# Routing of the first experts: row tables as single-row operations, work moved behind the ids, first hidden product moved ahead of the shares

## The reference

```
x = x + xattn(layernorm(x), ctx, mask)       # 16 heads, 77 context rows, 2048 tokens, width 256
h = layernorm(x)
scores = sigmoid(h @ gate.T + bias)           # 9 experts
top_scores, selected = top_k(scores, 2); top_scores /= sum(top_scores)
out = x + sum_e cw[:, e] * ((silu(h @ w1[e].T) * (h @ w3[e].T)) @ w2[e].T)   # hidden width 704
```

## Time and profile before

| what | value |
| --- | --- |
| median of 3 runs | 422.93 us (422.58 to 423.85) |
| profiled execution: own time | 422.82 us |
| its span (first to last instruction) | 421.0 us |
| mean granted PE clock | 0.989 |
| busy share of the span | PE 96%, DVE 65%, ACT 60%, POOL 59% |

### The profile page before, as it was taken

One profiled execution on the slowest core, in us unless ns is written; L12 is line 12 of the kernel. 1 busy time (PEld: TensorE's weight loads), 2 busy tenths in 40 slices (PEclk: granted clock), 3 DMA queues, 4 the chain that ended last, 5 costly groups with the idle time before them and its releaser, 6 DMA issues.

```text
span 421.0 us, 10140 instructions
## 1 busy us (share of the span) xinstructions
PE 403.9 (96%) x3176; PEld 307.2 (73%) x3176; DVE 275.2 (65%) x683; ACT 253.2 (60%) x444; POOL 246.9 (59%) x214
## 2 busy tenths in 40 slices
PE   8999999999999999789899999999999999999991
PEld 7777677778877877776677777777777777777781
DVE  1777989999899988987889854444444444444430
ACT  3759899999999986724655444444444444444430
POOL 6536789998999888253245534445444444444232
PEclk9999999999999999989999999999999999999997
DMA  7994456576575666256789978989889989989742
GB/s 228 342 321 132 132 160 201 161 189 201 155 235 166 177 187 190 74 151 120 154 138 139 146 131 133 141 139 129 150 141 142 141 139 140 143 134 153 119 68 36
DMA packets 106512, 66.03 MB, mean 157 GB/s; under 512 B 80992, under 2 KB 99808, under 8 KB 106464
## 3 DMA queue, kind: packets, MB, share of 16 engines
q1 hardware_dynamic: 98784, 54.90, 57.4%
q0 software_dynamic: 7680, 10.49, 16.5%
HBM read 36.23 MB, written 9.96 MB: 110 GB/s over the span
## 4 chain that ended last, share of the span: by engine, by line
PE 56%; issue 16%; DMA 14%; DVE 4%; POOLq 4%; POOL 3%; SPq 1%; ACT 0%; DVEq 0%
PE ps L824 12%; PE ps L621 12%; PE ps L651 11%; DMA out_rows<-work,idx_all 9%; PE ps L844 7%; PE ps L634 4%; POOLq L1709 3%; PE ps L558 3%; POOL work L1700 3%; PE ps L617 2%; DMA w_all<-in_wv 2%; PE ps L523 1%; DMA work<-work 1%; PE ps L667 1%; DMA work<-xn_rows,idx_all 1%
## 5 line engine op out<-in xcount | busy, mean ns | idle before, releaser
L824 PE MATMUL ps<-w_all,work 128*128 x960 | 150.1, 313 | 0.8 <-DVE work L1447 0.5
L824 PEld LDWEIGHTS ps<-w_all,work 128*128 128x128 f16 x960 | 93.6, 98 | 47.0 <-issue 1.2
L1721 POOL DMA_INDIRECT out_rows<-work,idx_all x40 | 64.2, 1606 | 102.5 <-ACT work L1076 101.1
L1516 DVE SCALAR_TENSOR_TENSOR work<-ps,work 128x352 f32<-128x352 f32 x80 | 41.2, 523 | 66.4 <-PE ps L824 66.3
L844 PE MATMUL ps<-w_all,work 128*128 x681 | 80.8, 273 | 1.1 <-DMA work<-work 1.1
L844 PEld LDWEIGHTS ps<-w_all,work 128*128 128x128 f16 x681 | 66.3, 98 | 12.0 <-issue 1.6
L1641 POOL TENSOR_TENSOR w_all<-stage,w_all 128x1088 f16<-128x1088 f32 x31 | 69.9, 2256 | 6.5 <-ACT w_all L916 6.2
L1055 ACT ACTIVATE work<-ps 128x352 f32<-128x352 f32 x80 | 36.8, 463 | 53.6 <-PE ps L824 53.6
L1061 ACT ACTIVATE work<-work 128x704 f16<-128x704 f32 x39 | 30.8, 790 | 62.2 <-DVE work L1516 62.2
L1700 POOL DMA_INDIRECT work<-xn_rows,idx_all x40 | 40.6, 1014 | 29.9 <-issue 10.3
L621 PE MATMUL ps<-w_all 128*128 128x462 f16 (+1 forms) x288 | 57.4, 336 | 0.0
(11 more groups left out here) (159 smaller groups left out, 537.2 us busy)
## 6 DMA issues: line engine op xcount, KB each, us to landing
stage<-in_wt SPq DMA_DIRECT2D x36, 544.0 KB, 4.4
work<-in_x SPq DMA_DIRECT2D x30, 128.0 KB, 3.7
out_rows<-work SPq DMA_DIRECT2D x18, 128.0 KB, 4.3
xn_rows<-work SPq DMA_DIRECT2D x18, 128.0 KB, 4.1
w_all<-in_x SPq DMA_DIRECT2D x1, 1536.0 KB, 14.6
work<-work SPq DMA_TRANSPOSE x78, 3.6
w_all<-in_wq SPq DMA_DIRECT2D x4, 256.0 KB, 6.8
w_all<-in_wv SPq DMA_DIRECT2D x2, 512.0 KB, 8.2
```

Source lines behind the costliest of these rows:

```text
L824: mm = pe.matmul(ps[:, c, 0:half], xt[:, t % 2, block, :], weights(wbase + off, half), start=(k == 0 and n == 0), stop=(k == KD - 1 and n ...
L1516: dve.scalar_tensor_tensor(out=sg[:, t % 2, cols], in0=ps[:, 2 + c, 0:HID // 2], scalar=1.0 / SP_W, in1=sg[:, t % 2, cols], op0=ALU.mult, ...
L1721: pool.indirect_dma_start(out=acc, out_offset=bass.IndirectOffsetOnAxis(ap=idx_all[:, t:t + 1], axis=0), in_=yb[:, t % 2], in_offset=None, ...
```

## The change

Five edits, all between the end of the attention loop and the third expert tile:

1. The 22 rows of `vhot1` are written by 22 `tensor_scalar` operations of 128 elements, each compared with a scalar per partition, in place of two `tensor_tensor` operations of 1408 elements. `pi` is first copied to a float table `pif`.
2. The two one-hot operations of `experts_of` become one of twice the width (both routings).
3. `stats` and `aggregate` of tile 13 go from ahead of `first_slots` to behind `ids_of(0)`; `normalise2(13)` goes behind `aggregate(14)` and the first `w_rest`, `rstd(13)` goes behind the gathers of tiles 0 and 1 in POOL's queue. `logits(11)` goes behind `residual(14)`.
4. On PE `gate_turn(12)` goes behind `first_ids`, `gate_logits(12)` into `project(15)`, `gate_turn(13)` behind `project(15)`, `gate_logits(13)` into up(0); ACT's `gate_copy(12)` goes behind the two table loads, `gate_copy(13)` behind `first_high`. The fillers become 8, 0 and 26 in place of 30, 16 and 10.
5. On DVE `normalise2(15)` and `shares(0)` go behind `hidden(0)`, and `logits(13)` ahead of step 0.

```diff
@@ PE
-        WARM, WARM_IDS, WARM_OUT, WARM_X0 = 30, 30, 16, 10
+        WARM, WARM_IDS, WARM_X0 = 30, 8, 26
...
                     if i == NT - 1 and c == G_AT:
-                        gate_turn(NT - 3)
+                        gate_logits(NT + 1 - LAG_G)
...
                 prob_turn(NT - 1)
-                gate_turn(NT + 1 - LAG_G)
                 pe.wait_ge(sub_ok, 3 * NT)
                 warm(WARM_IDS, WARM_LATE)
                 first_ids()
-                gate_logits(NT + 1 - LAG_G)
-                warm(WARM_OUT, WARM_LATE)
+                gate_turn(NT + 1 - LAG_G)
                 project(NT - 1)
-                gate_logits(NT - 3)
+                gate_turn(NT - 3)
...
-                if s in (1, 2):
+                if s in (0, 1, 2):
                     gate_logits(NT - 3 + s)
@@ ACT
-            gate_copy(NT + 1 - LAG_G)
             sigmoids(0, K1)
             act.activation(mx[:, 0, 0:1], eps[:], ACT.Silu)
+            gate_copy(NT + 1 - LAG_G)
+            first_high()
             gate_copy(NT - 3)
-            first_high()
@@ DVE, experts_of
-                for k in range(2):
-                    ins = dve.tensor_tensor(oh[:, k], by_expert(con[:, C_IOTA:C_IOTA + E9], n),
-                                            idx[:, k].unsqueeze(2).to_broadcast([P, n, E9]), ALU.is_equal)
-                link(ins)
+                link(dve.tensor_tensor(oh, by_expert(con[:, C_IOTA:C_IOTA + E9], n).unsqueeze(1).to_broadcast([P, 2, n, E9]),
+                                       idx.unsqueeze(3).to_broadcast([P, 2, n, E9]), ALU.is_equal))
@@ DVE, first_rows
+                dve.tensor_copy(r["pif"][:, :, 0:K1], r["pi"][:, :, 0:K1])
...
                 for k in range(2):
-                    row_hot(vhot1[:, k * K1:(k + 1) * K1, :], r["pi"][:, k, 0:K1], K1).then_inc(v1_ok, 1)
+                    for i in range(K1):
+                        ins = dve.tensor_scalar(vhot1[:, k * K1 + i, :], iota16[:], r["pif"][:, k, i:i + 1], None, ALU.is_equal)
+                    ins.then_inc(v1_ok, 1)
@@ DVE, drain
-                stats(NT - 3)
-                aggregate(NT - 3)
                 first_slots()
-                logits(NT - LAG_G)
                 first_rows()
                 residual(NT - 2)
+                logits(NT - LAG_G)
                 first_index()
                 p_low(NT - 1)
                 ids_of(0)
-                normalise2(NT - 3)
+                stats(NT - 3)
+                aggregate(NT - 3)
                 logits(NT + 1 - LAG_G)
                 stats(NT - 2)
                 aggregate(NT - 2)
                 w_rest(4 * EARLY + 3)
+                normalise2(NT - 3)
                 w_rest(4 * E9 - 4)
                 first_low()
-                logits(NT - 3)
@@ DVE, fstep
                     normalise2(NT - 2)
-                if n == 0:
-                    normalise2(NT - 1)
-                    shares(0)
+                    logits(NT - 3)
...
                     hidden(n)
                 if n == 0:
+                    normalise2(NT - 1)
+                    shares(0)
                     first_values()
@@ POOL
-                if on(n, LAG_X1):
+                if on(n, LAG_X1) and n < NT:
                     rstd(n - LAG_X1)
...
                 if n == -1:
+                    rstd(NT - 3)
                     rstd(NT - 2)
```

More of the change, by code:

```diff
@@ L238, in build @@
             ("sel", [2, NT, E9], F32), ("sgm", [2, NT], F32), ("wsum", [NT], F32), ("wrec", [NT], F32),
-            ("cwv", [2, NT], F32), ("sl", [2, NT], F32), ("sli", [2, NT], I32), ("pi", [2, NT], I32), ("ti", [2, NT], I32),
+            ("cwv", [2, NT], F32), ("pif", [2, NT], F32), ("sli", [2, NT], I32), ("pi", [2, NT], I32), ("ti", [2, NT], I32),
             ("val", [2, 2, NT], F16), ("pad", [NF2], F32), ("cws", [NF2], F32),
```

## The result

The changed kernel takes 425.6 us (median of 13 runs, 424.13 to 429.77), the kernel before 423.17 (13 runs, 421.91 to 423.85, same chip). The ratio is 1.0067 with a 95% interval of 1.0051 to 1.0083: slower by 2.4 us by the medians and by 2.8 by the ratio. The prediction was 422.1, with a range from 420.4 to 424.0. It was wrong in sign, and the time lies outside the range.

The account below looks back on a forecast made before the run. It took the start of down(0), set by first_turn through a chain of waits, as the bound. Rows starting 0.62 us sooner and costing 0.88 less bring ids 1.50 sooner, first_turn 0.75 after low clock and fillers: 422.1 us, range 420.4 to 424.0.

Parts of the forecast that it names:

- The price of a row: Row tables on DVE: 22 operations at 0.10 us each, 2.2 in place of 3.08, a gain of 0.88.
- its own sum: Whole kernel: 0.8 us earlier at first_turn, down(0) and the end, giving 422.1 us.
- its reading of L1223: DVE row with per-partition scalars, 0.32 us for 256 elements: taken to give about 0.19 a row, the upper bound.
- The other bound: Row tables on DVE: lower bound of 0.09 us a row, from a pair of 22-element operations, 2.0 in all.
- Whatever first_turn gains, down(0) gains: Chain from first_turn through gather 2 to down(0): the gain of 0.75 us passes on while PE keeps 1 us of slack.
- Rival 1: PE clock stays up through project(15): first_turn 2.4 us earlier, time 420.6; chance 0.22.
- The low stretch: PE at clock 0.50 from 179.90 to 183.30 again, some 3.4 us inside project(15).
- rival 3: Low clock lasts to first_turn on PE: first_turn at 188.7, 2.2 us later, time 425.2; chance 0.07.
- the one-hot: DVE ahead of the rows: two operations, together 0.43 us, become one of 0.36, a gain of 0.07.
- the -0.55 for the statistics: DVE ahead of the rows: stats and aggregate of tile 13 leave, so the rows start 0.55 us sooner.
- edit 5 at nothing: DVE's queue to h_low(0): hidden(0) ahead of normalise2(15) and shares(0) changes nothing, 4.4 us as before.
- the links of the chain: Waits that set down(0): first_turn, gather of tile 2 (3.82 us), DVE's queue, transposing DMA of hidden tile 0 (4.74).

Follow-up runs that it names:

- e12: Kernel before plus 30 extra tensor_scalar operations at its start, five each of six forms (width, type, scalar); one run, 423.38 us.
- e1: Kernel before with only the rows written as 22 single-row operations, with the copy to pif; ratio 1.0032, 424.11 us.
- e17: Kernel before with the moved work alone (edits 2, 3 and edit 4's gate moves), wide rows and old fillers; ratio 1.0041, 424.05 us.
- e4: Changed kernel with the last two weight loads behind the stores of step 0; ratio to the kernel before 1.0109, 426.79 us.
- e11: Kernel before with the last two weight loads moved behind the transposing DMA of tile 1 and two stores; ratio 0.9985, 422.16 us.
- e14: Kernel before with both the gap-closing fillers of e10 and the moved loads of e11; ratio 0.9946, 421.31 us.
- e15: The kernel of e7 with the last two weight loads moved as in e11; ratio to the kernel before 0.9989, 422.96 us.
- e13: Changed kernel with the last two weight loads behind the transposing DMA of tile 1 and two stores; ratio to the kernel before 1.0090, 427.64 us.
- e3: Changed kernel with fillers closing PE's gaps (30, 20, 5 and 26); ratio to the kernel before 1.0045, 424.33 us.
- e10: Kernel before with fillers alone changed to 30, 20 between the halves of first_ids, 0 and 10; ratio 1.0007, 423.32 us.
- e16: Kernel before with the first of the last two weight loads waiting for both w_rest; ratio 0.9993, 422.96 us.
- e6: Changed kernel with the first w_rest and normalise2(13) ahead of logits(12) on DVE; ratio to the kernel before 1.0055, 425.49 us.
- e9: Changed kernel with tile 12's gate operations and logits(11) in their old places; ratio to the kernel before 1.0047, 424.81 us.
- e2: Changed kernel with the two wide row operations put back; ratio to the kernel before 1.0050, 424.74 us.
- e8: Kernel before with only normalise2(15) and shares(0) moved behind hidden(0) on DVE; ratio 1.0006, 423.33 us.
- e5: Kernel before with only the filler counts changed, to 8, 0 and 26; ratio 1.0016, 424.09 us.
- e18: Kernel before with the single-row operations and the 8, 0 and 26 fillers together; ratio 1.0054, 424.77 us.
- e7: Changed kernel with wide rows, 30, 20, 5 and 10 fillers and e6's order on DVE; ratio to the kernel before 1.0032, 424.92 us.

## Why the prediction was wrong

At up(3) the forecast is off by 3.76 us (-0.75 against +3.01). The steps, with what each is off by:

1. **The price of a row: 1.38.** The prediction took 0.10 from a range of 0.09 to 0.19; the profile after has 0.163 and e12 0.164. It named 0.135 as the price from which the edit loses, and with 0.163 in place of 0.10 its own sum gives 422.1 + 22 x 0.063 = 423.5: slower, but still inside its range, so steps 2 and 3 carry the rest. The step that failed here is its reading of L1223 (where, besides, 0.32 - 0.14 is 0.18 and not 0.19): it took that row for a slow rate of elements and then set it aside because of its 4-byte data. In fact the rate is fast and the scalar has a fixed price, which hits the short rows hardest. The other bound, a pair of operations with constants, had no such scalar at all. e1 shows the rows slower than the wide form with nothing else changed.
2. **The landing of gather 2: 1.04.** "Whatever first_turn gains, down(0) gains" took its 3.82 us as fixed. In the trace, gather 2 landed 0.5 us behind the second load in both kernels, and later by 2.39 us in the changed one, as the load did by 2.40. The chain splits this into 1.35 for first_turn and 1.04 for the landing. That is an account and not two causes: both `w_rest`, and so the loads, also stand behind the rows in DVE's queue (e1: loads 0.58 later, first_turn 0.60). With the last loads near, fx_low(2) came 4.2 to 7.0 us behind gather 2, whether first_turn was at 17.2 (e17) or 20.6; with the loads behind it, at 3.3 to 3.5 in e4, e11 and e14, and at 4.0 and 4.9 in e15 and e13. So an earlier first_turn was mostly given back (e3, e10, e16, e17: fx_low(2) from 24.93 to 25.43), and a rival that said so was missing. Rival 1, the clock that stays up, happened in e3 and e10 and brought no gain over before.
3. **SP's queue, not costed.** The new place of `gate_logits(12)` makes DVE's `logits(12)` wait 1.36 us, and both `w_rest` stand behind it: the first of the last loads went out 2.45 us later (19.81) and the second, by the trace, 1.96 later. By the prediction's own times for DVE (first `w_rest` done at 183.6, `normalise2(13)` behind it) the first would have gone out near 17 on this scale. In the old order both `w_rest` ran from 183.25 on, behind a `logits(12)` that had not waited. The prediction followed this wait to first_low, where DVE's slack does cover it, and not to SP. e6 and e9 bring the loads forward by 1.2 to 1.4 and the landing back to 4.2; that the one causes the other is likely from the landings under e16, and not shown.
4. **Smaller terms ahead of project(15): 0.52.** The rows started 0.22 later than forecast. L1275, off by 0.17, is most of it: freed of the statistics of tile 13, it comes 0.5 us sooner, at 171.12, and meets a POOL operation that lasts to 171.46. The other 0.30 lies between the rows and project(15), with `logits(11)` now in front of `first_index`.
5. **The clock: 0.19 at first_turn.** The low stretch was twice as long as forecast, 6.9 us, but 2.6 of it lay ahead of project(15), where PE waits anyway. From the start of project(15) to first_turn the forecast was 6.63 and the trace shows 6.82. The mechanism and nearly the size were right; rival 3 did not happen.
6. **Behind fx_low(2): 0.63.** DVE's queue to h_low(0) is 0.22 longer: L1362 took 0.39 instead of 0.17 beside the issue of a gather. turn_tokens(3) to up(3) took 0.41 longer, since PE came to up(3) 1.27 us after that DMA had landed before, and now waits for it, if it is as in e2 and e6.

The sizes make 3.76. Right were the one-hot (0.37 for 0.43), the -0.55 for the statistics, edit 5 at nothing (e8), and the links of the chain: first_turn, gather 2, DVE's queue, the transposing DMAs, and PE full from there on.

By edits, alone in the kernel before: rows 1.0032, fillers 1.0016, moved work 1.0041, shares 1.0006. They would add up to 1.0095, and the whole is 1.0067. The four intervals together are wide enough (about 0.003 either way) that a plain sum can't be told from an overlap.

**What stays open.** What sets the landing of gather 2 beyond the spacing to the loads: e5 took 5.55 us with 3.7 us of spacing, and e15 and e13 took 4.0 and 4.9 with the loads behind. One suspect has no run of its own. In all eight kernels with 8, 0 and 26 fillers (changed, e2, e4, e5, e6, e9, e13, e18) the trace has one packet of 16 KB on an instruction queue at 23.1 to 24.2 us from the start of the drain, while gather 2 is under way (at 23.11 for 1.71 us in e5, at 23.37 for 0.96 in e13). In no other kernel is there one between 19 and 27. So the filler counts may cost something that has nothing to do with the clock. Why the changed kernel loses from later loads where the kernel before gains: e13's profile shows a wait for it, one execution of a kernel whose runs lie 5.4 us apart. What makes the clock fall in one execution of the kernel before and not in the next is open too. With fillers in the gap it fell less often: 11 of 12 executions of e10 and all 7 of e14 have a mean clock of 0.992 or more, against 56 of 113 of the kernel before.

## What to carry to other kernels

Price a short operation by a row of its own form, scalar operand included: in 22 operations of 128 elements the scalar cost more than the elements. When an edit makes a transfer start earlier, list which other transfers run then, and cost each queue behind a new wait, down to the DMAs that hang on it: here an earlier gather gained nothing until the loads beside it were moved, and moving them gained nothing sure until the clock was held. Two edits that are each worth nothing may be worth 2 us together, if each uncovers what the other one frees.

## What the runs showed of the hardware

- A scalar per partition costs a DVE `tensor_scalar` 0.06 us, at 64 and at 128 elements of 2 bytes and at 64 of 4 bytes (e12).
- DVE and POOL hold each other up. POOL's L1649 has one element: 0.19 us alone (182.66), 1.16 from 184.73 on while `w_rest` runs on DVE, ending 0.05 behind it. DVE's L1275 took 0.38 instead of 0.21, ending 0.04 behind the POOL operation. It took 0.37 or 0.38 in e2, e3, e6, e7, e9 and e17, all of which move the statistics, and 0.21 in e1. The Trainium skill ("SBUF — State Buffer", Who interferes with whom) says that the two share a port pair, which the first to issue keeps for the whole instruction; all three rows agree.
- 20 fillers (1.28 us) between the halves of `first_ids` and 30 ahead of them kept the clock at 1.00 in the profiles of e10 and e14, where the kernel before fell to 0.50 and the changed kernel, with 8 there, did for 6.9 us. The profiles of e11, e12 and e16, without the 20, did not fall either, so the mean clocks of all executions, told above, carry more.
- A gather of 128 rows (its rows in use 3.3 to 3.5 us after its issue in e4, e11 and e14) took up to 7.0 beside two loads of 544 KB (e17). The DMA share while it was under way was 0.86 to 1.01 with the loads (before, changed, e12) and 0.36 without (e14), and in none of twelve profiles did it land ahead of the second load.
